# Second attention of an audio tower: another order on TensorE, ScalarE and VectorE, with the values' product in two halves

## The chip, the cores and the metric

The kernel runs on one core of one Trainium2 chip. The metric is the device time of one execution in microseconds (us), from the host's timing of the chip; a profile of one execution gives the spans below. TensorE (PE) does the matmuls, VectorE (DVE) and ScalarE (ACT) read its results from PSUM, GpSimd (POOL) works on SBUF alone, and SyncE (SP) issues DMAs.

## The reference, cut to what matters

The whole kernel computes tokens from 16 signals, and two layers of attention and experts on them. The change lies in the second attention, which for 16 batches (`Bb`) of 255 tokens (`Nn`), 64 channels and 8 heads of 8 channels computes:

```python
qk = (x @ Wqk.T).reshape(Bb, Nn, 2, Hh, hd)
q = qk[:, :, 0].transpose(0, 2, 1, 3)
k = qk[:, :, 1].transpose(0, 2, 1, 3)
patch_score = jax.nn.softmax(jnp.einsum('bhnd,bhmd->bhnm', q, k) * scale, axis=-1)
...
attn = (1.0 - g) * patch_score + g * pos_score[None]
...
v = (x @ Wv.T).reshape(Bb, Nn, Hh, hd).transpose(0, 2, 1, 3)
out = jnp.einsum('bhnm,bhmd->bhnd', attn, v)
out = out.transpose(0, 2, 1, 3).reshape(Bb, Nn, Cc)
return out @ Wproj.T + bproj
```

The softmax over the positions (`pos_score`) does not depend on the tokens; its product with the values is worked out ahead of the loop.

## The kernel before

The second attention (`attention1_and_experts1`) goes through 64 units of work. A unit is one pair of heads of one batch; four units make a batch, two batches one pass of the loop on each engine. Nothing schedules them: each engine has a function `slot`, called once per unit, that says in what order the engine does its part, and semaphores join the engines. A slot on TensorE works on several units at once, each at another stage. The four slots of a batch are slot 0 to 3 (`p` in the code), and a slot's own unit is U. On TensorE a slot before the change is, in this order:

- **scores** (line 1557) of unit U + 1, four matmuls into one pair of PSUM banks, after VectorE has taken the maxima of unit U out of them;
- **turned scores** (line 1563) of unit U - 1, with keys on the partitions, from queries that carry the maxima as extra rows; ScalarE then takes their exponential (line 1920);
- **stack** (line 1551): the queries and keys of unit U + 3 gathered by six matmuls; ScalarE copies them out (lines 1894, 1896);
- **turned maxima** (line 1616) of unit U. VectorE adds them to the queries (line 2095);
- in slots 1 and 3 **outputs** (line 1573): exponentials times values for two units, contracted over 128 and then 127 keys, 16 matmuls in the records (float32 goes in two), in column tiles of 32; ScalarE copies them out in slots 0 and 2 (line 1914);
- in slot 3 the **batch's end**: the projection of the batch before (line 1579) and the **turned outputs** of this one (line 1585);
- in slot 2 the **turned blend** (line 1639) and the **next projection**, which makes queries and keys of the batch after next (line 1545).

VectorE's slot is: maxima of unit U + 1 (line 2062), the sum of queries and turned maxima of unit U (2095), the high and low parts of the new maxima (2071, 2072). Slot 1 adds statistics for a later normalisation (447 to 455), slot 3 a rest of queries and keys (2058) and the batch's end: reciprocals of the turned outputs' sums (2108, 2109), the blend (2112), and the sum with the projection (2119). The turned maxima share PSUM bank 7 with the turned outputs, so they wait in slot 0 until the blend has read those (`s_otr`).

Of the kernel before, what the change touches and what calls it, by code (L numbers as in the profile page):

```python
# [17 lines left out]
ALU = mybir.AluOpType  # L18
# [7 lines left out]
P = 128  # L26
# [8 lines left out]
D = WIN  # L35
# [52 lines left out]
def tower(nc, x, taps, consts, w_raw, gate_b0, w1_01, b1_0, w2_0, b2_0, gamma,  # L88
          split_sel, wpos, wproj, bproj, b1_1, w2_1, b2_1, out):
    with ExitStack() as ctx:  # L90
# [1350 lines left out]
        def attention1_and_experts1(block, e0):  # L1441
# [93 lines left out]
            def _(pe):  # L1535
# [45 lines left out]
                def outputs_turn(b, par):  # L1581
# [4 lines left out]
                    last.then_inc(s_OT, 1)  # L1586

                def slot(j, k, do=("unit", "turned", "pv", "tail")):
# [6 lines left out]
                    if "unit" in do and (not known or U + 1 < UNITS):  # L1595
# [3 lines left out]
                        scores(k + 1)  # L1599
                    if "turned" in do and (not known or U >= 1):  # L1600
# [10 lines left out]
                    if "unit" in do:  # L1611
                        pe.wait_ge(s_mhl, U + 1)
                        if p == 0 and (not known or b >= 2):
                            pe.wait_ge(s_otr, b - 1)
                        for tq in range(2):
                            last = nc.tensor.transpose(MT[:, P * tq:P * tq + P], mhl[k % 2][:, tq], ident_b[:])
                        last.then_inc(s_mtp, 1)
                    if "pv" in do and p % 2 == 1 and (not known or U >= 3):
# [131 lines left out]
                with pe.Fori(1, B // 2 - 1) as j:  # L1750
# [138 lines left out]
            def _(act):  # L1889
# [14 lines left out]
                def slot(j, k, do=("unit", "exp", "o")):  # L1904
# [3 lines left out]
                    b = 2 * j + par  # L1908
                    if p % 2 == 0 and (not known or b >= 1) and "o" in do:
# [5 lines left out]
                    if "exp" in do and (not known or U >= 1):  # L1915
# [593 lines left out]
```

## Time and profile before

| what | value |
|---|---|
| device time, median of 3 runs | 746.05 us (745.96 to 749.63) |
| span of the profiled execution | 745.7 us |
| TensorE busy in the span | 652.7 us (88%) |
| VectorE busy | 570.2 us (76%) |
| ScalarE busy | 502.8 us (67%) |
| GpSimd busy | 334.1 us (45%) |

The span runs from the first to the last instruction of the profiled execution; the median lies 0.35 us above it. The shares are over the whole kernel; the second attention is the stretch from about 494 to 660 us, and only there does an instruction move.

### The profile page before, as it was taken

Reading aid. Unit: us, or ns where it says so; the run is one execution under the profiler, and the core shown is the slowest. Engines: PE = TensorE matmul, PEld = TensorE weight load, DVE = VectorE, ACT = ScalarE, POOL = GpSimd, SP = SyncE. Lnnn points to the kernel's source line nnn. Section 1 sums busy time; section 2 is a strip of 40 time slices with the busy share of each in tenths; the row PEclk is TensorE's granted clock in tenths of the full one; section 3 lists DMA queues with packets and bytes.
Section 4 is the critical chain, followed back from the end, with each engine's and each line's share of the span. In section 5 each row is a group of like instructions: output and inputs, shape, how many; then the busy total and the mean of one; then the engine's idle time right before and its main releaser. Section 6 shows DMA issues by size and latency. Waiting matters only on the chain.

```text
span 745.7 us, 16401 instructions
## 1 busy us (share of the span) xinstructions
PE 652.7 (88%) x4984; PEld 364.3 (49%) x4984; DVE 570.2 (76%) x1633; ACT 502.8 (67%) x1264; POOL 334.1 (45%) x417
## 2 busy tenths in 40 slices
PE   5528998999999988999999997699888988889896
PEld 5514654666666654323333324365555655565332
DVE  6676787777777774798999988669888888867653
ACT  3746877888888872576777767658777777744542
POOL 1006578788787875133333333725445644320000
PEclk9857999999999997999999999699999999987999
DMA  4030000000000001433333330000000000000001
GB/s 109 1 113 1 1 2 1 0 0 0 0 0 0 1 0 66 161 106 108 109 113 115 107 109 14 3 1 2 1 0 0 0 0 0 1 1 1 16 20 23
DMA packets 22038, 24.37 MB, mean 33 GB/s; under 512 B 12390, under 2 KB 12902, under 8 KB 21734
## 3 DMA queue, kind: packets, MB, share of 16 engines
q1 hardware_dynamic: 19751, 23.31, 10.3%
q10 hardware_dynamic: 2239, 0.49, 0.3%
q8 instruction: 22, 0.36, 0.2%
q14 instruction: 26, 0.21, 0.1%
HBM read 22.48 MB, written 1.31 MB: 32 GB/s over the span
## 4 chain that ended last, share of the span: by engine, by line
PE 59%; DVE 19%; issue 8%; ACT 4%; POOL 2%; DMA 1%; DVEq 0%; SPq 0%; ACTq 0%; POOLq 0%
PE ps L723 8%; PE ps L759 7%; PE ps L1551 5%; PE ps L641 4%; PE ps L1573 4%; PE ps L717 4%; DVE big L1091 4%; PE ps L652 3%; DVE big L2062 3%; DVE big L1132 2%; PE ps L1557 2%; PE ps L1802 2%; PE ps L709 2%; PE ps L1824 2%; PE ps L705 2%
## 5 line engine op out<-in xcount | busy, mean ns | idle before, releaser
L1338 POOL TENSOR_TENSOR big<-big 128x1024 f32<-128x1024 f32 x64 | 119.9, 1895 | 45.3 <-DVE big L1152 45.3
L939 ACT ACTIVATE big<-ps,big 128x255 f32<-128x255 f32 x256 | 117.3, 485 | 11.4 <-DVE big L1146 8.9
L901 ACT ACTIVATE big<-ps,b1s 128x512 f32<-128x512 f32 x128 | 80.3, 679 | 40.1 <-PE ps L641 38.9
L1146 DVE TENSOR_REDUCE big<-ps 128x4 f32<-128x1020 f32 x64 | 75.2, 1213 | 27.3 <-PE ps L717 27.3
L1920 ACT ACTIVATE big<-ps 128x1024 f32<-128x1024 f32 x64 | 65.9, 1030 | 32.9 <-PE ps L1563 30.5
L2062 DVE TENSOR_REDUCE big<-ps 128x4 f32<-128x1020 f32 x64 | 78.1, 1220 | 6.8 <-DVE res L2119 2.5
L723 PE MATMUL ps<-cst,big 128*128 128x128 f32 x512 | 77.5, 285 | 6.3 <-POOL big L1338 2.4
L1158 DVE COPY mid<-ps 128x512 f32<-128x512 f32 x96 | 63.5, 686 | 18.7 <-PE ps L723 15.4
L641 PE MATMUL ps<-big,wall 64*128 64x512 f32 x256 | 75.7, 656 | 0.7 <-ACT big L872 0.7
L723 PEld LDWEIGHTS ps<-cst,big 128*128 128x128 f32 x512 | 54.9, 141 | 40.8 <-issue 20.8
L652 PE MATMUL ps<-big,w2s 128*64 128x512 f32 x256 | 70.8, 632 | 1.2 <-ACT big L901 1.2
L759 PE MATMUL ps<-mid,big 128*64 128x256 f32 (+1 forms) x512 | 69.5, 392 | 0.0
L1132 DVE SCALAR_TENSOR_TENSOR big<-ps,b2s,mid 128x512 f32<-128x512 f32 x64 | 48.0, 750 | 21.2 <-DMA mid<-spread_w 7.7
L939 ACT ACTIVATION_READ_ACCUMULATOR big<-ps,big 128x1 f32 x256 | 55.7, 217 | 0.0
L465 POOL TENSOR_TENSOR big<-big 128x4 f32<-128x4 f32 x16 | 16.3, 1016 | 85.6 <-DVE big L455 85.6
L1551 PE MATMUL ps<-big,selqk 128*128 128x256 bf16 x384 | 52.8, 273 | 0.7 <-ACT big L1896 0.4
L1091 DVE TENSOR_TENSOR big<-big 128x512 f32<-128x512 f32 x56 | 44.1, 788 | 0.0
L927 ACT ACTIVATE big<-ps 128x512 f32<-128x512 f32 x64 | 35.0, 602 | 11.1 <-PE ps L705 8.9
L460 POOL TENSOR_TENSOR mid<-mid 128x2 f32<-128x2 f32 x16 | 11.5, 718 | 66.5 <-DVE mid L455 66.5
L1551 PEld LDWEIGHTS ps<-big,selqk 128*128 128x128 bf16 x384 | 32.8, 97 | 17.2 <-issue 13.5
L1557 PE MATMUL ps<-big 64*128 64x256 bf16 x256 | 25.4, 273 | 17.8 <-DVE big L2062 17.7
L759 PEld LDWEIGHTS ps<-mid,big 128*64 128x64 f32 (+1 forms) x512 | 31.1, 136 | 18.7 <-issue 7.9
(274 smaller groups left out, 1342.2 us busy)
## 6 DMA issues: line engine op xcount, KB each, us to landing
mid<-spread_w SPq DMA_DIRECT2D x128, 128.0 KB, 2.8
mid<-in_split_sel SPq DMA_DIRECT2D x1, 1536.0 KB, 7.5
wall<-in_w SPq DMA_DIRECT2D x1, 1280.0 KB, 6.2
out_tokens<-res SPq DMA_DIRECT2D x16, 56.0 KB, 1.6
cst<-in_consts SPq DMA_DIRECT2D x1, 520.5 KB, 5.1
pexp<-in_w_raw SPq DMA_DIRECT2D x1, 512.0 KB, 6.2
w2s<-in_w SPq DMA_DIRECT2D x1, 512.0 KB, 3.4
mid<-in_taps ACTq DMA_DIRECT2D x1, 320.0 KB, 3.9
```

What stands on the lines that cost most here:

```text
L641: last = nc.tensor.matmul(H1(e, j), wst[0][half, f:f + P], xc[q][half], start=True, stop=True)
L652: last = nc.tensor.matmul(Y(e)[D * j:D * j + D], w2s[0][:, 2 * e + j], hid[e % 2][j], start=True, stop=True)
L723: last = nc.tensor.transpose(AT[:, j, c, P * tq:P * tq + P], e_sb[r % 4][:, j, tq, P * c:P * c + P], ident)
L759: last = nc.tensor.matmul(O[D * j:D * j + D, par], val[par][0:n, c, D * h:D * h + D], a_sb[r % 4][0:n, j, c], start=(g == 0 and a == 0 and ...
L901: last = nc.scalar.activation(hid[e % 2][j], H1(e, j), ACT.Relu, bias=b1s[0][:, 2 * e + j:2 * e + j + 1])
L939: last = nc.scalar.activation(e_sb[r % 4][:, jj, tq, 0:NW], S[:, 2 * (r % 2) + jj, tq, 0:NW], ACT.Exp, scale=-1.0, bias=minus[r % 4][:, jj ...
L1091: ins = nc.vector.tensor_tensor(acc[q], acc[q], part[e % 2], ALU.add)
L1146: nc.vector.tensor_reduce(minus[r % 4], S[:, 2 * a:2 * a + 2, :, 0:NW], AX.X, ALU.min).then_inc(s_mx, 1)
L1338: nc.gpsimd.tensor_tensor(e_sb[r % 4], e_sb[r % 4], bc(inverse[r % 4].unsqueeze(3), [P, 2, 2, 256]), ALU.mult).then_inc(s_A, 1)
L1551: last = nc.tensor.matmul(out_, selqk[:, 2 * p + n, part], parts[par][:, part], start=(part == 0), stop=(part == 2))
L1920: nc.scalar.activation(e_sb[(k - 1) % 4], T, ACT.Exp, scale=scale).then_inc(s_E, 1)
L2062: nc.vector.tensor_reduce(mx[k % 2], S[:, :, :, 0:NW], AX.X, ALU.max).then_inc(s_max, 1)
```

## The change

On TensorE the turned maxima go from behind the stack to between scores and turned scores, except in slot 1. The outputs product is cut into its two contractions: the first 128 keys in slots 1 and 3, the other 127 in the slot behind. The batch's end goes from slot 3 to slot 0 of the next batch, behind the second half; the turned maxima of slot 1 are done last in their slot and wait for the blend. On VectorE the batch's end goes from the end of slot 3 to slot 1, between the maxima and the sum with the queries, and the rest of queries and keys goes behind the parts. On ScalarE the copy of the outputs goes from ahead of the exponential to behind it. TensorE's loop starts one pass later; that pass is written out.

```diff
@@ TensorE @@
-                def outputs(k):
+                def outputs(k, c):
...
                     g = p // 2
-                    for c in range(2):
-                        n = P - c
-                        for i in range(4):
-                            last = nc.tensor.matmul(O[32 * i:32 * i + 32, g], v1[par][0:n, c, 4 * g + i], e_sb[(k + i // 2) % 4][0:n, i % 2, c],
-                                                    start=(c == 0), stop=(c == 1))
-                    last.then_inc(s_PV, 1)
+                    n = P - c
+                    for i in range(4):
+                        last = nc.tensor.matmul(O[32 * i:32 * i + 32, g], v1[par][0:n, c, 4 * g + i], e_sb[(k + i // 2) % 4][0:n, i % 2, c],
+                                                start=(c == 0), stop=(c == 1))
+                    if c == 1:
+                        last.then_inc(s_PV, 1)
...
+                def batch_end(b, par):
+
+                    if not isinstance(b, int) or b + 2 < B:
+                        pe.wait_ge(s_rest, b + 3)
+                    if not isinstance(b, int) or b >= 2:
+                        projected(b)
+                    if not isinstance(b, int) or b <= B:
+                        outputs_turn(b, par)
+
+                def max_turn(U, k):
+                    pe.wait_ge(s_mhl, U + 1)
+                    if not isinstance(U, int) or U >= 1:
+                        pe.wait_ge(s_qm, U)
+                    for tq in range(2):
+                        last = nc.tensor.transpose(MT[:, P * tq:P * tq + P], mhl[k % 2][:, tq], ident_b[:])
+                    last.then_inc(s_mtp, 1)
...
                         scores(k + 1)
+                    if "unit" in do and p != 1:
+                        max_turn(U, k)
                     if "turned" in do and (not known or U >= 1):
...
-                        outputs(k - 3)
-                    if p == 3 and (not known or b >= 1) and "tail" in do:
-                        if not known or b + 2 < B:
-                            pe.wait_ge(s_rest, b + 3)
+                        outputs(k - 3, 0)
+                        if known and U >= UNITS - 1:
+                            outputs(k - 3, 1)
+                    if "pv" in do and p % 2 == 0 and (not known or 4 <= U < UNITS):
+                        outputs(k - 4, 1)
+                    if p == 1 and "unit" in do:
+                        if not known or b >= 2:
+                            pe.wait_ge(s_otr, b - 1)
+                        max_turn(U, k)
+                    if p == 0 and "unit" in do and (not known or b >= 2):
+                        pe.wait_ge(s_qm, U + 1)
+                        batch_end(b - 1, 1 - par)
+                    if known and p == 3 and b >= B - 1 and "tail" in do:
                         if "unit" in do:
                             pe.wait_ge(s_qm, U + 1)
-                        if not known or b >= 2:
-                            projected(b)
-                        if not known or b <= B:
-                            outputs_turn(b, par)
+                        batch_end(b, par)
...
@@ ScalarE @@
+                    if "exp" in do and (not known or U >= 1):
+                        act.wait_ge(s_T, U)
...
+                        nc.scalar.activation(e_sb[(k - 1) % 4], T, ACT.Exp, scale=scale).then_inc(s_E, 1)
                     if p % 2 == 0 and (not known or b >= 1) and "o" in do:
...
-                        nc.scalar.activation(e_sb[(k - 1) % 4], T, ACT.Exp, scale=scale).then_inc(s_E, 1)
@@ VectorE @@
                             maxima(U + 1, k + 1)
-                        if p == 3 and (not known or b + 2 < B):
-                            remains(b + 2, par)
+                        if p == 1 and (not known or b >= 2):
+                            batch_end(b - 1)
+                        if p == 1 and (not known or b >= 3):
+                            dve.wait_ge(s_fin, b - 2)
                         dve.wait_ge(s_mtp, U + 1)
...
                             max_parts(U + 1, k + 1)
+                        if p == 3 and (not known or b + 2 < B):
+                            remains(b + 2, par)
...
-                    if p == 3 and (not known or 1 <= b <= B):
-                        dve.wait_ge(s_OT, b)
-                        link(nc.vector.reciprocal(rinv, by_head[:, :, :, HS - 1]))
...
-                        dve.wait_ge(s_fin, b - 1)
+                    if known and p == 3 and b >= B - 1:
+                        batch_end(b)
```

The next two pieces are TensorE's instructions around the batch's end in a pass of the loop, with their semaphores (`L1_` and the name of what has been done). Before, from the outputs of slot 3 to the first matmul of the stack of slot 0:

```order
L1573 MATMUL ps<-big,mid 32x256 [waits L1_outputs_in_sbuf,L1_values_padded]
L1573 MATMUL ps<-big,mid 32x256 x7
L1579 MATMUL ps<-wps,big 128x128 [waits L1_blend_in_sbuf,L1_q_with_max,L1_qk_rest]
L1582 REGISTER_ALU
L1585 MATMUL ps<-cst,big 128x128 [waits L1_outputs_in_sbuf]
L1585 MATMUL ps<-cst,big 128x128 x3
L1557 MATMUL ps<-big 128x256 [waits L1_max,L1_k_in_sbuf,L1_q_in_sbuf]
L1557 MATMUL ps<-big 128x256 x3
L1563 MATMUL ps<-big 128x256 [waits L1_exps,L1_q_with_max]
L1563 MATMUL ps<-big 128x256 x3
L1608 REGISTER_ALU
L1551 MATMUL ps<-big,selqk 128x256 [waits L1_k_in_sbuf,L1_q_in_sbuf]
```

The outputs (1573) stand whole in slot 3, the batch's end (1579, 1585) behind them; in slot 0 the turned scores (1563) follow the scores (1557), and the turned maxima come later, behind the stack (1551).

After, slot 0 behind its scores, up to the turned outputs (the lines of the same work are 1602 for the turned maxima and 1572 for outputs):

```order
L1602 MATMUL ps<-ident_b,big 128x128 [waits L1_q_with_max,L1_max_parts]
L1602 MATMUL ps<-ident_b,big 128x128
L1563 MATMUL ps<-big 128x256 [waits L1_exps,L1_q_with_max]
L1563 MATMUL ps<-big 128x256 x3
L1627 REGISTER_ALU
L1551 MATMUL ps<-big,selqk 128x256 [waits L1_k_in_sbuf,L1_q_in_sbuf]
L1551 MATMUL ps<-big,selqk 128x256 x5
L1572 MATMUL ps<-big,mid 32x256 x4
L1579 MATMUL ps<-wps,big 128x128 [waits L1_blend_in_sbuf,L1_qk_rest,L1_q_with_max]
L1582 REGISTER_ALU
L1585 MATMUL ps<-cst,big 128x128 [waits L1_outputs_in_sbuf]
L1585 MATMUL ps<-cst,big 128x128 x3
```

The turned maxima now stand ahead of the turned scores, half of the outputs (four of the eight instructions) behind the stack, and the batch's end (1579, 1585) in slot 0 with a wait for VectorE's sum (`L1_q_with_max`).

After, slot 1 behind its scores, up to the turned maxima of slot 2:

```order
L1563 MATMUL ps<-big 128x256 [waits L1_exps,L1_q_with_max]
L1563 MATMUL ps<-big 128x256 x3
L1627 REGISTER_ALU [waits L1_parts_ready]
L1551 MATMUL ps<-big,selqk 128x256 [waits L1_k_in_sbuf,L1_q_in_sbuf]
L1551 MATMUL ps<-big,selqk 128x256 x5
L1635 ISA [waits L1_exps]
L1572 MATMUL ps<-big,mid 32x256 [waits L1_outputs_in_sbuf]
L1572 MATMUL ps<-big,mid 32x256 x3
L1602 MATMUL ps<-ident_b,big 128x128 [waits L1_q_with_max,L1_max_parts,L1_turned_outputs_read]
L1602 MATMUL ps<-ident_b,big 128x128
L1557 MATMUL ps<-big 128x256 [waits L1_max,L1_k_in_sbuf,L1_q_in_sbuf]
L1557 MATMUL ps<-big 128x256 x3
```

Here the turned maxima (1602) stand last and wait for the blend (`L1_turned_outputs_read`); the scores of slot 2 and their turned maxima follow at once.

VectorE before, from the parts in slot 3 to the first maxima of the next batch's slot 0:

```order
L2071 TENSOR_TENSOR big<-big 128x4 [waits L1_max_turned,L1_max]
L75 REGISTER_ALU
L2072 TENSOR_TENSOR big<-big 128x4 [waits L1_dve]
L2108 RECIPROCAL big<-ps 128x16 [waits L1_outputs_turned]
L2109 TENSOR_TENSOR big<-big,tail 128x16 [waits L1_dve]
L75 REGISTER_ALU
L2111 REGISTER_ALU [waits L1_dve]
L2112 TENSOR_TENSOR big<-ps,big 128x128 [waits L1_blend_turned]
L2119 ISA [waits L1_projected]
L2119 TENSOR_TENSOR res<-res,ps 128x128
L2061 REGISTER_ALU [waits L1_added]
L2062 TENSOR_REDUCE big<-ps 128x4 [waits L1_scores]
```

The maxima (2062) of slot 0 wait behind the batch's end.

After, slot 1 from its maxima to the first of the parts:

```order
L2082 TENSOR_REDUCE big<-ps 128x4 [waits L1_scores]
L2106 ISA
L2107 RECIPROCAL big<-ps 128x16 [waits L1_outputs_turned]
L75 REGISTER_ALU
L2108 TENSOR_TENSOR big<-big,tail 128x16 [waits L1_dve]
L75 REGISTER_ALU
L2110 REGISTER_ALU [waits L1_dve]
L2111 TENSOR_TENSOR big<-ps,big 128x128 [waits L1_blend_turned]
L2118 ISA [waits L1_projected]
L2118 TENSOR_TENSOR res<-res,ps 128x128
L2135 TENSOR_TENSOR big<-big,ps 128x256 [waits L1_turned_scores,L1_max_turned,L1_added]
L2091 TENSOR_TENSOR big<-big 128x4 [waits L1_max_turned,L1_max]
```

The five instructions of the batch's end (2107 to 2118, before 2108 to 2119) stood ahead of the maxima (2062) of a slot 0; they now stand behind the maxima (2082) of slot 1 and ahead of the sum with the queries (2135).

## Rows read from the trace of the kernel before

**Rows 1.** Busy us (count) of PE, PEld, DVE, ACT, POOL; clock; DMA: one batch.

```profile
599.17:609.45 10.28, 9.10 (x106) 5.97 (x107) 8.99 (x29) 7.75 (x16) 4.98 (x9) 1.00 0.00 0
```

**Rows 2.** Chain that ended last: scores of slot 1, first and last of thirteen.

```profile
515.88 0.40 PE ps L1557 x4
...
640.60 0.40 PE ps L1557 x4
```

**Rows 3.** Timeline, TensorE, one batch from slot 1: start, us, line, shape, count [idle before].

```profile
599.17 0.40 PE L1557 MATMUL ps<-big 64*128 64x256 bf16 x4 [1.49 <-DVE big L2062]
599.39 0.40 PE L1563 MATMUL ps<-big 64*128 64x256 bf16 x4
599.72 0.83 PE L1551 MATMUL ps<-big,selqk 128*128 128x256 bf16 x6
600.39 0.28 PE L1616 MATMUL ps<-ident_b,big 128*128 128x128 bf16 x2
600.59 1.07 PE L1573 MATMUL ps<-big,mid 128*32 128x256 f32 x16
601.60 0.40 PE L1557 MATMUL ps<-big 64*128 64x256 bf16 x4
...
602.81 0.28 PE L1616 MATMUL ps<-ident_b,big 128*128 128x128 bf16 x2
602.92 0.28 PE L1639 MATMUL ps<-cst,big 128*128 128x128 f32 x1
603.04 0.49 PE L1545 MATMUL ps<-big,w 128*128 128x256 bf16 x3
603.46 0.40 PE L1557 MATMUL ps<-big 64*128 64x256 bf16 x4
...
605.93 0.49 PE L1579 MATMUL ps<-wps,big 128*128 128x128 f32 x2
606.25 0.60 PE L1585 MATMUL ps<-cst,big 128*128 128x128 f32 x4
606.78 0.40 PE L1557 MATMUL ps<-big 64*128 64x256 bf16 x4
```

**Rows 4.** Timeline, VectorE, the same batch.

```profile
599.61 1.22 DVE L2062 TENSOR_REDUCE big<-ps 128x4 f32<-128x1020 f32 x1
600.75 0.28 DVE L2095 TENSOR_TENSOR big<-big,ps 128x256 bf16<-128x256 bf16 x1
...
601.15 0.18 DVE L2072 TENSOR_TENSOR big<-big 128x4 bf16<-128x4 f32 x1
601.30 0.36 DVE L447 BATCH_NORM_STATS2 mid<-res 128x6 f32 x2
...
602.09 1.22 DVE L2062 TENSOR_REDUCE big<-ps 128x4 f32<-128x1020 f32 x1
...
606.89 0.26 DVE L2108 RECIPROCAL big<-ps 128x16 f32<-128x16 f32 x1 [0.61 <-PE ps L1585]
...
607.48 0.29 DVE L2112 TENSOR_TENSOR big<-ps,big 128x128 f32<-128x128 f32 x1
607.69 0.28 DVE L2119 TENSOR_TENSOR res<-res,ps 128x128 f32 x1
608.09 1.22 DVE L2062 TENSOR_REDUCE big<-ps 128x4 f32<-128x1020 f32 x1
```

**Rows 5.** Timeline, the last batch: scores of slot 1, then a wait, last turned scores.

```profile
650.70 0.40 PE L1557 MATMUL ps<-big 64*128 64x256 bf16 x4 [1.01 <-DVE big L2062]
...
654.63 0.28 DVE L2095 TENSOR_TENSOR big<-big,ps 128x256 bf16<-128x256 bf16 x1
...
654.96 0.40 PE L1563 MATMUL ps<-big 64*128 64x256 bf16 x4 [1.50 <-DVE big L2095]
...
657.36 0.40 PE L1563 MATMUL ps<-big 64*128 64x256 bf16 x4
```

**Rows 6.** Busy us by stretch, as rows 1: behind the second attention.

```profile
668.00:676.00 8.00, 8.00 (x35) 7.24 (x36) 6.16 (x43) 1.45 (x4) 0.71 (x1) 0.50 0.00 0
```

More of the change, by code:

```diff
@@ L1610, in slot @@
                         stack(at(k + 3)[0], at(k + 3)[1])
[L1611 to L1617, printed above, removed]
                     if "pv" in do and p % 2 == 1 and (not known or U >= 3):
@@ L1749, in _ @@
                     slot(0, k)
-                with pe.Fori(1, B // 2 - 1) as j:
+                for k in range(2 * PAIRS):
+                    slot(1, k)
+                with pe.Fori(2, B // 2 - 1) as j:
                     for k in range(2 * PAIRS):
@@ L2080, in scale_twice, with batch_end @@
                     dve.wait_ge(s_nx, b + 1)
+                def batch_end(b):
+                    known = isinstance(b, int)
+                    if not known or 1 <= b <= B:
+                        dve.wait_ge(s_OT, b)
+                        link(nc.vector.reciprocal(rinv, by_head[:, :, :, HS - 1]))
+                        link(nc.vector.tensor_tensor(rgate, rinv, omg, ALU.mult))
+                        if not known or b >= 2:
+                            dve.wait_ge(s_oTp, b - 1)
+                        nc.vector.tensor_tensor(blend.rearrange("p t (h d) -> p t h d", h=H), by_head[:, :, :, 0:HS - 1],
+                                                bc(rgate.unsqueeze(3), [P, 2, H, D // H]), ALU.mult).then_inc(s_otr, 1)
+                    if not known or b >= 2:
+                        if known and b == 2:
+                            dve.wait_ge(s_biased, CH)
+                        dve.wait_ge(s_y, b - 1)
+                        rs = res[:, span(2 * (b - 2), 2)]
+                        nc.vector.tensor_tensor(rs, rs, Y, ALU.add).then_inc(s_fin, 1)
                 def slot(j, k, do=("unit",)):
@@ L2105, in slot @@
                         scale_twice(b - 3)
-                    if p == 3 and (not known or 1 <= b <= B):
-                        dve.wait_ge(s_OT, b)
-                        link(nc.vector.reciprocal(rinv, by_head[:, :, :, HS - 1]))
-                        link(nc.vector.tensor_tensor(rgate, rinv, omg, ALU.mult))
-                        if not known or b >= 2:
-                            dve.wait_ge(s_oTp, b - 1)
-                        nc.vector.tensor_tensor(blend.rearrange("p t (h d) -> p t h d", h=H), by_head[:, :, :, 0:HS - 1],
-                                                bc(rgate.unsqueeze(3), [P, 2, H, D // H]), ALU.mult).then_inc(s_otr, 1)
-                    if p == 3 and (not known or b >= 2):
-                        if known and b == 2:
-                            dve.wait_ge(s_biased, CH)
-                        dve.wait_ge(s_y, b - 1)
-                        rs = res[:, span(2 * (b - 2), 2)]
-                        nc.vector.tensor_tensor(rs, rs, Y, ALU.add).then_inc(s_fin, 1)
-                        dve.wait_ge(s_fin, b - 1)
+                    if known and p == 3 and b >= B - 1:
+                        batch_end(b)
                 def values_out(c):
```

8 lines of the change are left out of this document (4 added, 4 removed).

## The prediction

> **What bounds the kernel now.** I read the busy time by stretch first, then the chain that ended last, then TensorE's and VectorE's instructions in order of time, and last the end of the stage. In one batch of the second attention, 10.28 us, TensorE is busy 9.10, VectorE 8.99 and ScalarE 7.75, at a granted clock of 1.00 (2.4 GHz) [rows 1]. So TensorE and VectorE each have little over 1 us spare, and the batch is as long as it is because the two wait for each other. The chain shows the pace: from the scores at 515.88 to the same scores twelve batches later at 640.60 are 124.72 us, **10.39 per batch** [rows 2]. Where the waiting lies is in the next two views. TensorE stood 1.49 us for VectorE before the scores at 599.17, and from there to 606.78 shows no wait [rows 3]. VectorE stands 0.61 until the outputs are turned, then does the batch's end from 606.89, and only then, at 608.09, begins the next maxima [rows 4]. The next scores need those maxima's result, so TensorE pays for the batch's end. What could be gained is this wait, 1.49 us here.
>
> The four slots of a batch are numbered 0 to 3, as in the section on the kernel; rows 3 begin with slot 1.
>
> **A price that the steps need: changing the tile shape.** TensorE's rows carry the shape (64\*128, 128\*128, 128\*32). Start to start, equal shapes follow at streaming pace: scores to turned scores 0.22, turned maxima to turned blend 0.11, turned blend to projection of the next batch 0.12. Where the shape changes, about 0.1 is added: turned scores to stack 0.33 against 0.22; turned maxima to outputs 0.20 against 0.11; the three matmuls of the next batch's projection to scores 0.42 against three times 0.11; the turned outputs to scores 0.53 [rows 3]. I take **0.10 per change**. The Trainium skill has a rule that speaks against this change: TensorEngine Tiling (Array Packing), section Key Properties, says that a change of tiling mode (not only of tile) drains TensorE. The rows agree with a cost per change. That page has no price; TensorE: Matmul & The Clock Gate, section Step-by-step: what each phase is for, gives about 128 cycles for the last column to leave the array, and its section on LDWEIGHTS 107 ns for 128 columns, so an estimate from the skill would be 0.16 per change, and the sum below would be about 8 us higher by it.
>
> **The change, walked through one batch.** Zero is the start of the scores in slot 1; all steps are start to start. From rows 3: scores to a 128-row shape 0.32 (0.22 and a change), turned maxima to turned scores 0.21 (0.11 and a change), turned scores to stack 0.33, stack to half an outputs product 0.77 (0.67 and a change), the half to anything else 0.56 (the whole takes 1.01 with one change, so 0.46 and a change), projection 0.32, turned outputs 0.53, turned blend 0.12, next projection 0.42.
>
> Slot 1. TensorE: scores, turned scores, stack, half, ending at 0.22 + 0.33 + 0.77 + 0.56 = 1.88. Then it must turn the maxima, and now waits until VectorE has read the turned outputs. VectorE: maxima from 0.44, the next instruction 1.14 later (599.61 to 600.75), so the batch's end starts at 1.58; reciprocal to blend 0.59, blend 0.29 long: read at 2.46 [rows 4]. A VectorE result releases TensorE after 0.05 (sum of queries and maxima 654.63 to 654.91, turned scores at 654.96 [rows 5]): the maxima are turned at **2.51**, 0.63 after TensorE was free. This is the old wait's successor. Behind it on TensorE stand the scores, turned scores and stack of slot 2.
>
> Slot 2. TensorE's scores at 2.72, ready for the turned maxima at 3.04. VectorE adds the maxima to the queries once they are turned (0.28 long, 0.05 to release: 2.84), ends their high and low parts 0.40 + 0.18 later [rows 4], 3.42; TensorE turns them at **3.47**, another 0.43 lost. VectorE's statistics then start at 3.39 and the maxima 0.79 later [rows 4], at 4.18, ready for TensorE at 4.18 + 1.22 + 0.14 = 5.54 (0.14 from the maxima at 608.09, 1.22 long, to the scores at the boundary 609.45 of the window [rows 1, 4]). TensorE needs 0.21 + 0.33 + 0.77 + 0.56 + 0.12 + 0.42 = 2.41, so slot 3 begins at **5.88**: TensorE is the later one.
>
> Slot 3: 0.32 + 0.21 + 0.33 + 0.77 + 0.56 = 2.19, to **8.07**. Slot 0 of the next batch: 0.32 + 0.21 + 0.33 + 0.77 + 0.56 + 0.32 + 0.53 = 3.04, to **11.11**. VectorE meanwhile has 1.80 to do per slot (0.44 + 1.22 + 0.14) and is early in both, so the wait of 1.49 is indeed gone; but slots 0 and 3 are now TensorE's own work, with four or more changes in each where two or three stood. ScalarE's moved copy of outputs waits for the second half, but ScalarE has 10.28 - 7.75 = 2.5 us spare [rows 1], so I cost it, GpSimd's add (4.98 busy [rows 1]) and the longer code (the first passes of the loop are written out) at nothing; without that cover the copy is priced below.
>
> **The sum.** A batch goes from 10.39 to 11.11: +0.72, twelve times, **+8.6**. The batch after (640.60 to 650.70, 10.10 [rows 2, 5]) has no projection of a next batch: by the same steps slot 3 begins at 5.56, the batch is 10.79, **+0.7**. The last batch takes 657.36 - 650.70 = 6.66 to its last turned scores [rows 5]. With the change VectorE's maxima there start at 4.18 as above, their parts end at 5.90, TensorE turns them at 5.95, then turned scores, both halves, projection, turned outputs, 0.21 + 0.33 + 1.01 + 0.32 + 0.53: 8.35, **+1.7**. The first two batches have no batch's end and come out within 0.1. Total +11.0. The span is 745.7 and the median 746.05, 0.35 around it; with that unchanged the forecast is **757 us**.
>
> **The rivals.**
> *Faster.* TensorE loads the next weights ahead whatever their shape, as long as it has work queued, and a change then costs nothing. Sixteen changes stand on the path from 3.47 to 11.11. Without them slot 3 begins at 5.54 (VectorE is the later one there), slot 3 takes VectorE's 1.80 and slot 0 takes 0.22 + 0.11 + 0.22 + 0.67 + 0.46 + 0.32 + 0.43 = 2.43: 9.77 per batch, -0.6 twelve times, +1 at the end: about 740 us. Against it: from 599.17 to 606.78 TensorE has work queued all the time, and each change costs its 0.1 [rows 3]. It comes out under the time before only if a change costs under 0.04.
> *No change.* Eleven of the sixteen changes are new (five stand in rows 3 already). If the new ones hide and the old ones do not, slot 3 begins at 5.58, slots 3 and 0 take 1.80 and 2.64: 10.02 per batch, -0.4 twelve times, +1.3 at the end: 743; if half of the new ones hide, 10.55 per batch and about 750.
> *Slower still.* The copy of outputs stands ahead of the copies of queries and keys on ScalarE; if it waits longer than my walk says, the next stack waits too. A wait of 0.27 in two slots of thirteen batches is +7: about 764.
> *The clock.* The stage behind runs at 0.50 (1.2 GHz) for long after the sparse end of this one [rows 6]; a longer sparse end may move this by a few us either way. It widens the range.
>
> **Chances.** Slower as worked out 0.66, slower still 0.11, no change 0.13, faster 0.10. A measurement of this kernel tells about 0.5% (3.7 us) from no change. So faster 0.10, same 0.13, slower 0.77. The range leaves out the faster case and the far end of slower still: 746 to 764. If slower as worked out holds, 751 to 763.
>
> **What would show it.** Right: the wait before the scores of slot 1 gone; 0.4 to 0.7 before the turned maxima of slots 1 and 2, released by VectorE's blend and parts; turned maxima between scores and turned scores with 0.32 and 0.21 to their neighbours; 11.0 to 11.2 from batch to batch; VectorE idle about 0.7 us more per batch. Wrong: scores to turned maxima at 0.22, or a batch of under 10.4, would bear out the faster rival; a stack that waits for ScalarE, the slower one.

## The result, and the profile after

After takes 765.69 us (759.10 to 771.07, 4 runs), before in the same comparison 746.76 us (745.96 to 749.63, 4 runs): ratio **1.0234** (95% interval 1.0190 to 1.0277). The four runs spread over 12 us with the granted clock of the whole kernel (0.954 in the fastest, 0.931 in the slowest, which the ratio leaves out). The change makes the kernel slower, as forecast, but by 17.5 us at that ratio (18.9 between the medians) and not by 11. The profiled execution took 764.48 us, its span is 761.7 us, 16.0 longer than before's 745.7.

First the busy time of one batch, from the scores of slot 1 to the same scores of the next batch, the answer to [rows 1]. The columns are busy us (count) of PE, PEld, DVE, ACT and POOL, then TensorE's granted clock, DMA share and GB/s.

```profile
606.73:617.99 11.26, 10.28 (x108) 5.16 (x108) 8.65 (x27) 7.91 (x18) 5.01 (x9) 1.00 0.00 0
```

TensorE is busy 10.28 us of 11.26, where it was 9.10 of 10.28: the same products, with the outputs in more pieces, at the same clock, keep it busy 1.18 us longer, and 0.98 is idle still. Now TensorE's instructions in that batch, the answer to [rows 3] (start, us, line, shape, count, idle time before and what ended it):

```profile
606.73 0.40 PE L1557 MATMUL ps<-big 64*128 64x256 bf16 x4
...
609.24 0.29 PE L1602 MATMUL ps<-ident_b,big 128*128 128x128 bf16 x2 [0.57 <-DVE big L2111]
609.45 0.39 PE L1557 MATMUL ps<-big 64*128 64x256 bf16 x4
610.26 0.28 PE L1602 MATMUL ps<-ident_b,big 128*128 128x128 bf16 x2 [0.41 <-DVE big L2092]
...
612.72 0.40 PE L1557 MATMUL ps<-big 64*128 64x256 bf16 x4
613.05 0.28 PE L1602 MATMUL ps<-ident_b,big 128*128 128x128 bf16 x2
613.27 0.40 PE L1563 MATMUL ps<-big 64*128 64x256 bf16 x4
...
614.93 0.40 PE L1557 MATMUL ps<-big 64*128 64x256 bf16 x4
...
617.99 0.40 PE L1557 MATMUL ps<-big 64*128 64x256 bf16 x4
```

The wait of 1.49 us before the scores of slot 1 is gone. Two others stand in its place: 0.57 before the turned maxima of slot 1, released by the blend (L2111), and 0.41 before those of slot 2, released by the parts (L2092). From slot 3 on nothing waits; there the chain of waits too runs along TensorE alone. VectorE in slot 1, the answer to [rows 4]:

```profile
607.17 1.22 DVE L2082 TENSOR_REDUCE big<-ps 128x4 f32<-128x1020 f32 x1 [1.15 <-PE ps L1557]
...
608.89 0.29 DVE L2111 TENSOR_TENSOR big<-ps,big 128x128 f32<-128x128 f32 x1
...
609.62 0.29 DVE L2135 TENSOR_TENSOR big<-big,ps 128x256 bf16<-128x256 bf16 x1 [0.24 <-PE ps L1602]
```

Now it is VectorE that stands 1.15 us for TensorE's scores. Over the batch it is idle 2.61 us (11.26 - 8.65), where it was 1.29 before: 1.32 more. 0.33 of that is the low part of the maxima, which took 0.51 us before, beside GpSimd's work (605.77), and takes 0.18 here.

The pace, which was 124.72 us for twelve batches [rows 2], is read here from the scores of slot 1 in TensorE's timeline: the batch that begins at 516.21, the one behind it, and the last but one.

```profile
516.21 0.40 PE L1557 MATMUL ps<-big 64*128 64x256 bf16 x4
...
528.28 0.40 PE L1557 MATMUL ps<-big 64*128 64x256 bf16 x4
...
651.58 0.40 PE L1557 MATMUL ps<-big 64*128 64x256 bf16 x4
```

135.37 us for the twelve, +10.65. The first takes 12.07, the other eleven 123.30, or 11.21 each. What the first meets is in the timeline of its slots 1 and 2:

```profile
518.95 0.29 DVE L2135 TENSOR_TENSOR big<-big,ps 128x256 bf16<-128x256 bf16 x1 [0.38 <-PE ps L1602]
519.06 2.77 POOL L2377 TENSOR_TENSOR res<-res,bprojb 128x256 f32<-128x256 f32 x4
519.16 0.66 DVE L2091 TENSOR_TENSOR big<-big 128x4 bf16<-128x4 f32 x1
519.85 0.65 DVE L2092 TENSOR_TENSOR big<-big 128x4 bf16<-128x4 f32 x1
...
520.56 0.28 PE L1602 MATMUL ps<-ident_b,big 128*128 128x128 bf16 x2 [1.31 <-DVE big L2092]
```

VectorE's two parts take 0.66 and 0.65 us instead of 0.17 and 0.18 while GpSimd adds a bias (L2377, four additions in 2.77 us), and TensorE's turned maxima wait 1.31 for them. In the kernel before, the same additions slowed the parts as much (0.69 and 0.65 at 515.85), but the turned maxima stood behind the stack there and came 0.2 later than else (scores of slot 1 to those of slot 2 in 2.63, in the next batch 2.42).

Last the end of the stage, the answer to [rows 5] and [rows 6]: busy time by stretch, and TensorE's timeline of the last batch.

```profile
664.00:665.00 1.00, 0.01 (x1) 0.01 (x1) 0.93 (x5) 0.26 (x1) 0.00 (x0) 1.00 0.00 0
665.00:666.00 1.00, 0.60 (x6) 0.22 (x6) 0.72 (x6) 0.00 (x0) 0.45 (x1) 1.00 0.00 0
666.50:667.00 0.50, 0.50 (x11) 0.20 (x8) 0.47 (x2) 0.33 (x1) 0.23 (x1) 0.51 0.00 0
...
670.00:672.00 2.00, 2.00 (x16) 1.10 (x9) 0.00 (x0) 0.38 (x1) 0.00 (x0) 0.50 0.00 0
672.00:673.00 1.00, 1.00 (x8) 0.48 (x6) 0.21 (x1) 0.00 (x0) 0.00 (x0) 0.50 0.00 0
...
680.60:697.40 16.80, 16.80 (x72) 12.56 (x72) 13.28 (x98) 4.84 (x9) 1.66 (x3) 0.51 0.01 1
```

```profile
662.57 0.40 PE L1557 MATMUL ps<-big 64*128 64x256 bf16 x4
...
664.99 0.28 PE L1602 MATMUL ps<-ident_b,big 128*128 128x128 bf16 x2 [1.24 <-DVE big L2111]
...
668.37 0.40 PE L1602 MATMUL ps<-ident_b,big 128*128 128x128 bf16 x2 [0.33 <-DVE big L2092]
668.69 0.61 PE L1563 MATMUL ps<-big 64*128 64x256 bf16 x4
669.24 1.93 PE L1572 MATMUL ps<-big,mid 128*32 128x256 f32 x16
...
672.68 0.61 PE L1563 MATMUL ps<-big 64*128 64x256 bf16 x4
674.78 1.07 PE L1572 MATMUL ps<-big,mid 128*32 128x256 f32 x16 [1.49 <-ACT big L1940]
```

TensorE stands still for 1.24 us in the last batch, is busy for 0.60 us of the microsecond from 665, and from 666.5 to 673 the granted clock is 0.50 (1.2 GHz): its last products run at half the clock, inside the attention. The last batch takes 10.11 us (662.57 to 672.68) where it took 6.66. In the kernel before, the clock stayed at 1.00 to the end of its last batch, at 657.36. The stretch at half clock in the stage behind is as long as before: here 680.6 to 697.4, there 664.6 to 681.3.

**Where the 16.0 us of span went.** To the scores of slot 1 of the batch at 516.21, from the first scores of slot 0 (495.06): 21.15 against 19.45, +1.70. The twelve batches: +10.65. The batch behind them: 10.99 against 10.10, +0.89. The last batch: +3.45. From its last turned scores to the last outputs: 2.10 (672.68 to 674.78) against 1.52, +0.58. Sum 17.3. The attention begins 1.37 earlier (495.06 against 496.43), which is not the change's doing: over the profiles of this document that start lies anywhere from 491.66 to 496.55. What stands behind the attention is 0.1 longer. 17.3 - 1.4 + 0.1 = 16.0.

### The profile page after: what moved, and what is told of

Read it like the earlier page. It is cut to its first block, busy times and chain, and to the rows that moved or that the text cites. A ratio compares the mean times of both kernels' runs of the same rounds, so it can differ in the third digit from the quotient of the medians.

```text
span 761.7 us, 16427 instructions
## 1 busy us (share of the span) xinstructions
PE 670.7 (88%) x4984; PEld 354.0 (46%) x4984; DVE 566.2 (74%) x1633; ACT 503.8 (66%) x1264; POOL 334.4 (44%) x417
## 3 DMA queue, kind: packets, MB, share of 16 engines
HBM read 22.48 MB, written 1.31 MB: 31 GB/s over the span
## 4 chain that ended last, share of the span: by engine, by line
PE 58%; DVE 18%; issue 9%; ACT 5%; POOL 2%; DMA 2%; SPq 0%; DVEq 0%; ACTq 0%; POOLq 0%
PE ps L723 8%; PE ps L759 7%; PE ps L1551 5%; PE ps L717 4%; PE ps L1572 4%; DVE big L1091 4%; PE ps L641 3%; PE ps L1563 2%; DVE big L1132 2%; PE ps L652 2%; PE ps L1557 2%; PE ps L1602 2%; PE ps L705 2%; PE ps L1844 2%; PE ps L709 2%
## 5 line engine op out<-in xcount | busy, mean ns | idle before, releaser
L641 PE MATMUL ps<-big,wall 64*128 64x512 f32 x256 | 73.6, 640 | 0.7 <-ACT big L872 0.7
L652 PE MATMUL ps<-big,w2s 128*64 128x512 f32 x256 | 69.0, 617 | 1.5 <-ACT big L901 1.2
L1572 PE MATMUL ps<-big,mid 127*32 127x256 f32 (+1 forms) x512 | 41.8, 402 | 1.5 <-ACT big L1940 1.5
L717 PE MATMUL ps<-big 32*128 32x256 f32 x512 | 37.6, 408 | 2.9 <-ACT big L939 1.7
```

The source lines that it names most:

```text
L641: last = nc.tensor.matmul(H1(e, j), wst[0][half, f:f + P], xc[q][half], start=True, stop=True)
L652: last = nc.tensor.matmul(Y(e)[D * j:D * j + D], w2s[0][:, 2 * e + j], hid[e % 2][j], start=True, stop=True)
```

## The experiments

Before, run beside them, took 746.10 us in the comparison of the first four experiments, 743.91 in that of the next four and 744.46 in that of the last. Per batch means from scores of slot 1 to scores of slot 1, and twelve batches means the stretch that took 124.72 us before. M is the new place of the turned maxima on TensorE, H the two halves of the outputs with ScalarE's copy behind the exponential, B the batch's end in the next batch with VectorE's part of it, and what goes with it (the turned maxima of slot 1 last in their slot, the rest of queries and keys behind the parts, the pass that is written out).

| kernel | ratio to before (95%) | twelve batches, us | head, us | last batch, us |
|---|---|---|---|---|
| before | 1 | 124.72 | 19.45 | 6.66 |
| after (M, H, B) | 1.0234 (1.0190 to 1.0277) | 135.37 | 21.15 | 10.11 |
| M alone | 1.0160 (1.0085 to 1.0236) | 133.39 | 21.18 | 6.97 |
| H alone | 1.0021 (0.9990 to 1.0052) | 126.62 | 19.87 | 6.67 |
| B alone | 1.0110 (1.0075 to 1.0144) | 129.34 | 19.81 | 7.90 |
| H and B (after without M) | 1.0111 (1.0028 to 1.0194) | 128.61 | 19.94 | 7.90 |
| M and B (after without H) | 1.0254 (1.0197 to 1.0311) | 132.88 | 21.22 | 10.11 |
| after, TensorE kept busy at the end | 1.0194 (1.0147 to 1.0240) | 135.41 | 21.15 | 8.96 |
| after, GpSimd's bias additions early | 1.0286 (1.0226 to 1.0347) | 134.39 | 21.15 | 10.10 |
| before, sum with projection behind the maxima | 0.9960 (0.9922 to 0.9998) | 118.97 | 19.44 | 6.67 |
| the same, projection in the next slot 0 | 0.9907 (0.9875 to 0.9940) | 116.04 | 19.45 | 6.67 |

Head is the stretch from the first scores of slot 0 to the first of the twelve batches.

Which slots the parts lengthen is read from the same timelines: us from the scores of a slot to those of the next, mean of the eleven batches behind the first of the twelve.

| kernel | slot 1 | slot 2 | slot 3 | slot 0 |
|---|---|---|---|---|
| before | 2.43 | 1.87 | 3.32 | 2.79 |
| M alone | 2.72 | 2.07 | 3.49 | 2.78 |
| H alone | 2.05 | 2.58 | 3.12 | 2.78 |
| B alone | 2.68 | 2.80 | 2.43 | 2.88 |
| H and B | 2.68 | 2.87 | 2.14 | 3.03 |
| M and B | 2.68 | 2.80 | 2.71 | 2.85 |
| after | 2.68 | 3.27 | 2.20 | 3.06 |

**The turned maxima alone (M).** Before, with this edit on TensorE, in all four slots (the change leaves out slot 1):

```diff
+                    if "unit" in do:
+                        pe.wait_ge(s_mhl, U + 1)
...
+                        last.then_inc(s_mtp, 1)
                     if "turned" in do and (not known or U >= 1):
                         pe.wait_ge(s_qm, U)
...
-                    if "unit" in do:
-                        pe.wait_ge(s_mhl, U + 1)
...
-                        last.then_inc(s_mtp, 1)
```

> The kernel before, with one part of the change alone: TensorE turns the maxima between scores and turned scores in every slot; the outputs stay whole and the batch's end stays in slot 3. Theory A (each change of tile shape on TensorE's path costs 0.10 us): two changes more in slots 1, 2 and 3, slot 0 covered by its wait; slots 1 to 3 take 2.7, 2.1 and 3.5 instead of 2.4, 1.9 and 3.3, the batch goes from 10.3/10.6 to 11.0/11.3, the kernel to about 755 us (ratio 1.011 to 1.013). Rival (the loss of the change is the new wait behind VectorE's batch end, the order on TensorE costs nothing): 10.3/10.6 per batch, ratio 0.998 to 1.002.

Measured: 10.95 and 11.25 per batch in turn, 758.70 us. In its timeline of TensorE, the start of slot 0, the start of slot 1, and the scores of slots 2, 3 and 0 read:

```profile
590.94 0.40 PE L1557 MATMUL ps<-big 64*128 64x256 bf16 x4
592.07 0.27 PE L1607 MATMUL ps<-ident_b,big 128*128 128x128 bf16 x2 [0.74 <-DVE big L2114]
...
593.61 0.40 PE L1557 MATMUL ps<-big 64*128 64x256 bf16 x4 [0.18 <-DVE big L2064]
594.01 0.28 PE L1607 MATMUL ps<-ident_b,big 128*128 128x128 bf16 x2
...
596.32 0.40 PE L1557 MATMUL ps<-big 64*128 64x256 bf16 x4
...
598.39 0.40 PE L1557 MATMUL ps<-big 64*128 64x256 bf16 x4
...
601.88 0.40 PE L1557 MATMUL ps<-big 64*128 64x256 bf16 x4
```

In slot 0 the turned maxima now stand in front of turned scores and stack, so these wait for the blend (L2114) as well, 0.74 us, which they did not before. That wait costs nothing: slot 0 takes 2.78 in the mean and took 2.79, since the scores of slot 1 wait for VectorE in both. The loss is in the other three: 2.71, 2.07 and 3.49 us here (593.61 to 601.88), where [rows 3] have 2.43, 1.86 and 3.32. That is two changes of shape more in each, and in slot 1 another 0.07 (scores to turned maxima 0.40 instead of 0.33). Theory A holds, slot for slot, and its rival falls. This part alone costs 8.67 us in twelve batches, and in the head 1.73, as much as the whole change does.

**The two halves alone (H).** The outputs cut in two as in the diff of the change, with ScalarE's copy behind the exponential; nothing else.

> The kernel before, with another part alone: the outputs product in two halves over two slots, ScalarE's copy of the outputs behind the exponential; turned maxima and batch's end stay where they were. Theory A: slots 1 and 3 get shorter by 0.45, slots 2 and 0 longer by 0.56; slot 0 has the old wait as cover, VectorE's maxima hold slot 2: 10.25 to 10.4 per batch, ratio 0.997 to 1.004. Rival (splitting is itself costly: a second change of shape and ScalarE's later copy on the path in both places): 10.7 or more per batch, ratio over 1.006.

Measured: 10.35 and 10.73 per batch in turn, 748.05 us: +1.90 in twelve batches, 10.55 per batch in the mean, and no difference that the times can tell. The ratio is Theory A's, and its interval (up to 1.0052) leaves the rival's out; per batch every second one lies where the rival had it, and the mean lies between the two. Slot 2 gets longer by 0.71 us, although VectorE was to hold it, and slot 3 shorter by 0.20 and not by 0.45; slot 0 stays covered, as Theory A said. Behind the last batch ScalarE's later copy shows:

```profile
660.76 1.07 PE L1572 MATMUL ps<-big,mid 128*32 128x256 f32 x16 [1.49 <-ACT big L1924]
```

The last outputs wait for that copy (L1924) and come 1.88 us behind the last turned scores at a clock of 1.00, where they came 1.52 behind before: 0.36 for the copy.

**The batch's end alone (B).** After, with the outputs whole again and the turned maxima behind the stack, except in slot 1, where they stay last.

> The kernel before, with the third part alone: the batch's end in slot 0 of the next batch on TensorE and in slot 1 on VectorE, the turned maxima of slot 1 last in their slot; outputs whole, turned maxima of the other slots behind the stack. Theory A: the old wait goes, in its place come 0.2 before the turned maxima and 0.4 before the turned scores of slot 2, and slot 3 begins at VectorE's 5.5; 10.7 to 10.9 per batch, ratio 1.005 to 1.009. Rival (the batch's end is the whole loss): 11.1 to 11.3 per batch, ratio 1.014 or more. A third way, that the removed wait counts and nothing takes its place: 9.4 to 9.8, ratio 0.985.

Measured: 10.62 to 11.07 per batch, 10.78 in the mean, 753.65 us. Theory A holds for the batch, and the rival falls; the ratio (1.0110) lies a little above its numbers. Moved without M, the batch's end lengthens the last batch by 1.24 us (7.90), and the clock there stays at 1.00.

**TensorE kept busy at the end.** To tell whether the last batch is long by its order or by the clock: after, with the last batches' stack repeated in the last four slots, results unread.

```diff
+                    if known and "turned" in do and UNITS - 3 <= U <= UNITS:
+                        pe.wait_ge(s_q, UNITS)
+                        pe.wait_ge(s_k, UNITS)
+                        again(2 if U == UNITS else 1)
```

> The changed kernel with four stacks more on TensorE at the end of the second attention (one behind the turned scores of each of the last three units, two behind the very last), written to the same PSUM and read by nobody: work added, none left out. Theory A (the clock fell in the last batch because TensorE did little there): the granted clock stays at 1.00 through the last batch, which takes 8.2 to 8.6 instead of 10.1 to the last turned scores, 2 us are won there, and if the half clock in the next stage goes as well, up to 8 more: 754 to 763. Rival (the clock falls whatever TensorE does there, or on the work of the whole stage): the clock is 0.50 for as long, the time is the changed kernel's 764 or up to 2 more.

Measured: 761.22 us. The windows and the end of the last batch:

```profile
664.00:666.00 2.00, 1.59 (x17) 0.85 (x16) 1.65 (x11) 0.44 (x1) 0.71 (x2) 1.00 0.00 0
666.00:668.00 2.00, 1.84 (x20) 0.71 (x18) 1.46 (x5) 1.22 (x4) 1.90 (x3) 1.00 0.00 0
...
681.50:705.00 23.50, 21.67 (x74) 11.27 (x73) 14.28 (x88) 8.77 (x15) 1.40 (x2) 0.50 0.00 1
```

```profile
661.46 0.40 PE L1557 MATMUL ps<-big 64*128 64x256 bf16 x4
...
667.26 0.28 PE L1608 MATMUL ps<-ident_b,big 128*128 128x128 bf16 x2 [0.15 <-DVE big L2102]
667.48 0.39 PE L1563 MATMUL ps<-big 64*128 64x256 bf16 x4
667.81 0.83 PE L1581 MATMUL ps<-big,selqk 128*128 128x256 bf16 x6
668.56 1.07 PE L1572 MATMUL ps<-big,mid 128*32 128x256 f32 x16
...
670.42 0.40 PE L1563 MATMUL ps<-big 64*128 64x256 bf16 x4
```

With TensorE at work in the gaps the clock stays at 1.00, as Theory A has it, and the last batch takes 8.96 us. Of these 0.75 are the repeated stack at 667.81, which nothing hides (668.56 - 667.48 = 1.08 where 0.33 stood): without it 8.21. So the order costs the last batch 8.21 - 6.66 = 1.55 us and the clock the other 1.90. In the next stage 1.2 GHz lasts here from 681.5 beyond 705, against 16.8 us in after. That the work in the gaps brought this is not shown: the profiled run (766.50 us, span 764.7) is the longest of its four, whose other spans are 757.0 to 760.8, and the first stretch at half clock in that stage lasts 10 to 17 us in the profiles of the other kernels. Nor do the times tell this kernel from after (1.0194 against 1.0234, with intervals that overlap). So it is shown that the half clock lengthens the last batch; that filling the gaps would make the kernel faster is not.

**The sum with the projection behind the maxima.** A version of before, on VectorE alone: reciprocals and blend stay where they were, only their sum with the projection goes behind the maxima of slot 0.

```diff
                     if "unit" in do:
+                        if p == 0 and (not known or b >= 2):
+                            gated(b - 1)
                         if not known or U + 1 < UNITS:
                             maxima(U + 1, k + 1)
+                        if p == 0 and (not known or b >= 3):
+                            added(b - 1)
```

> The kernel before on every engine but VectorE: reciprocals and blend of the batch's end stand at the start of slot 0 (so the loop's branch falls into the wait for the turned outputs), the sum with the projection goes behind slot 0's maxima. Theory A (what VectorE does between the turned outputs and the next maxima sets the batch, since TensorE's next scores wait for those maxima): 0.4 less in each batch and 0.3 more where the loop ends, 9.8 to 10.0 per batch instead of 10.39, the kernel at 739 to 742 us (ratio 0.99 to 0.994). Rival (TensorE's own work or ScalarE holds the batch at 10.3 once VectorE is earlier): 10.2 to 10.4 per batch, ratio 0.998 to 1.002.

Measured: 742.93 us and 9.86 to 10.03 per batch, twelve in 118.97 (-5.75). Per batch Theory A holds; the ratio (0.9960) lies a little above its 0.99 to 0.994, with an interval that just leaves out 1. VectorE's work between the turned outputs and the scores of slot 1 is on the path that sets the end of a batch; taking 0.4 us out of it is a gain in every batch, and moving the whole of it was not.

**GpSimd's bias additions early.** After, with the additions of L2377 put ahead of GpSimd's loop, to tell whether they cost the head and the batch at 516.21.

```diff
+                for c in range(CH):
+                    add_bias(c)
                 for b in range(B):
                     slots(b, b % 2)
...
-                    if b < 2:
-                        for c in range(CH // 2 * b, CH // 2 * b + CH // 2):
-                            add_bias(c)
```

> The changed kernel with GpSimd's eight additions of the projection's bias ahead of its batch loop instead of behind its first two batches. Theory A (VectorE's parts take 0.66 instead of 0.17 in slot 2 of batch 2 because GpSimd's additions run then, and the change has put them on the path): batch 2 takes 11.2 instead of 12.07, the first eleven units 0.5 to 1.5 less, the kernel 1.5 to 2.5 us less than the changed one. Rival (the first pass is slow for another reason, as the code that is now written out): batch 2 at 12.07 still, no difference.

Measured: the batch at that place takes 11.11 us instead of 12.07; its parts read

```profile
517.17 0.17 DVE L2091 TENSOR_TENSOR big<-big 128x4 bf16<-128x4 f32 x1
517.37 0.18 DVE L2092 TENSOR_TENSOR big<-big 128x4 bf16<-128x4 f32 x1
```

That 0.96 us is shown to be GpSimd's. The head stays at 21.15, where Theory A had 0.5 to 1.5 less: its 1.7 us are not GpSimd's. In the head the longest wait of TensorE is, in after and here, another:

```profile
506.62 0.82 PE L1551 MATMUL ps<-big,selqk 128*128 128x256 bf16 x6 [0.69 <-ACT big L1916]
```

This line of after is a stack that waits 0.69 us for ScalarE, the sign that the prediction gave for its slower rival; here the same wait ends at 504.63. From 516.21 on the timeline of after shows no stack that waits. The time does not show the gain (764.65 us, four runs between 760.23 and 769.95).

**After without M, and after without H.** Each is after with one part undone as in the kernels above.

> The changed kernel with the turned maxima behind the stack again in slots 0, 2 and 3; halves and moved batch's end stay. Theory A (changes of shape on the path, waits as walked): 10.5 to 10.8 per batch, ratio to before 1.004 to 1.01. Rival (the parts' losses add up, each alone 0.16 and 0.38 over before): 10.9 to 11.0 per batch.

Measured: 10.50 to 11.08 per batch, 10.72 in the mean, 755.80 us, last batch 7.90 at a clock of 1.00. Theory A holds per batch, and the rival falls. Without M, 6.8 of the 10.65 us in twelve batches, 1.2 of the head's 1.7 and 2.2 of the last batch's 3.45 are gone.

> The changed kernel with the outputs product whole in slots 1 and 3 and ScalarE's copy ahead of the exponential again; order of the turned maxima and moved batch's end stay. Theory A: slot 1 has the whole product in its wait, slot 3 begins at VectorE's 5.5: 10.9 to 11.05 per batch, ratio to before 1.012 to 1.018. Rival (the parts' losses add up, each alone 0.72 and 0.38 over before): 11.4 to 11.5 per batch.

Measured: 10.99 and 11.06 per batch for most, 762.56 us. Theory A holds per batch, and the rival falls (11.03 in the mean behind the first batch); the ratio (1.0254) lies above its numbers, which had no half clock in the last batch. That batch takes 10.11 with the half clock in it, so in these profiles the fall comes with M and B together, and H is not needed for it.

**The projection in the next slot 0.** On top of the fifth kernel: its trace still has 0.69 to 0.78 us of idle time before the scores of slot 1, and the projection stands ahead of the turned outputs. It goes into that idle time.

```diff
                         last.then_inc(s_mtp, 1)
+                        if p == 0 and (not known or b >= 3):
+                            projected(b - 1)
...
-                        if not known or b >= 2:
+                        if known and b >= B - 1:
                             projected(b)
+                        elif not known or b >= 2:
+                            pe.wait_ge(s_oT, b - 1)
```

> The kernel of the fifth experiment (sum with the projection behind slot 0's maxima on VectorE, 9.86 to 10.03 per batch), and on TensorE the projection taken out of slot 3 and put into slot 0 of the next batch, behind its turned maxima, where the trace of the fifth has 0.69 to 0.78 of idle time before the next scores. Theory A (what is left of the old wait is the way from the turned outputs over reciprocal, blend and maxima to the scores of slot 1, and the projection stands ahead of the turned outputs on it): turned outputs, reciprocal, blend, maxima and scores all come about 0.33 earlier, the projection costs nothing in the idle time: 9.55 to 9.65 per batch, span about 4 us less than the fifth's 738.0, ratio to before 0.985 to 0.992. Rival (VectorE's own work in slot 3, whose parts end 0.48 before the reciprocal, is next in the way, or the added projection pushes the scores): a batch of 9.75 to 9.95 and a ratio of 0.992 to 0.997.

Measured: 737.98 us, ratio 0.9907; 9.59 and 9.77 per batch in turn, span 733.9. TensorE's timeline at the end of slot 3 and in slot 0:

```profile
589.02 0.66 PE L1585 MATMUL ps<-cst,big 128*128 128x128 f32 x4
...
590.90 0.28 PE L1616 MATMUL ps<-ident_b,big 128*128 128x128 bf16 x2
591.01 0.44 PE L1579 MATMUL ps<-wps,big 128*128 128x128 f32 x2
591.97 0.40 PE L1557 MATMUL ps<-big 64*128 64x256 bf16 x4 [0.52 <-DVE big L2068]
```

The projection costs nothing behind the turned maxima: slot 0 takes 2.22 us in the mean, 2.21 in the fifth kernel. The ratio and the span, 4.1 us below the fifth's, are Theory A's, though the ratio's interval (up to 0.9940) reaches into the rival's; a batch takes 9.67 in the mean, 0.24 less than the fifth's and not 0.33, and every second one lies in the rival's range, so what holds those is open. 0.52 us are left in this batch of the wait that was 1.49 in [rows 3]. This is the fastest version that ran.

## Why the prediction was wrong in size

**Right: the mechanism and the batch.** The forecast's walk gave the turned maxima of slot 1 at 2.51, of slot 2 at 3.47, slot 3 at 5.88, slot 0 at 8.07, the end at 11.11. Measured from 606.73: 2.51, 3.53, 5.99, 8.20 and 11.26. The old wait is gone and the two new ones stand where it said, released by the instructions that it named. Per batch 11.21 was measured (eleven batches): 0.10 more than 11.11. One sign came out larger: VectorE is idle 1.32 us more per batch, not 0.7.

**Right: the price of a shape.** Scores to turned maxima take 0.33 and turned maxima to turned scores 0.22 (612.72 to 613.27), forecast 0.32 and 0.21. So the faster rival and no change fall at the point that the prediction set for them, 0.32 against 0.22; M alone adds 0.29, 0.20 and 0.17 us to slots 1 to 3 for two changes in each. The page TensorEngine Tiling (Array Packing) of the Trainium skill, section Key Properties, says that a change of tiling mode drains TensorE; these steps agree that each change costs something, and do not show by what. With the 0.16 per change of the prediction's other estimate the sum would have been 765, which is where the time came out, but by chance: a change costs 0.10 to 0.11 in these rows, and the rest came from elsewhere.

**Wrong: the last batch, "+1.7".** The step was worked out at the full clock, and at that clock it was right: 8.35 forecast, 8.21 in the kernel kept busy. In the kernel after, the turned maxima that it put at 5.95 come at 5.80 (668.37); what follows up to the last turned scores was 2.40 in the sum and is 4.31 (668.37 to 672.68), at 1.2 GHz. The clock adds 1.90 to this term. Behind it the last outputs come 0.58 later, which had no term: 0.36 is ScalarE's copy, as in H alone, and the other 0.22 comes with the half clock, as in M and B without H (1.74 against 1.52). The prediction had the clock as a rival that "widens the range" by a few us, and looked for it in the stage behind, whose half clock is as long as before; it fell in the batch itself, after waits of 1.24 us for the blend and 0.41 for the parts. A wait alone does not tell: before has one of 1.50 us in its last batch [rows 5], B alone one of 1.62, both at a clock of 1.00.

**Wrong: "The first two batches have no batch's end and come out within 0.1".** They took 1.70 more. The reason given was beside the point: the turned maxima in front need no batch's end to cost time. M alone has the head at 21.18, H and B alone have it at 19.87 and 19.81, H and B together at 19.94. What holds TensorE there is not the same in each: with M alone the longest wait of the head is 0.75 us for VectorE's parts, after has the 0.69 for ScalarE. That M brings the loss is shown; how much of it each wait makes is open.

**Wrong: GpSimd and ScalarE's copy "at nothing".** The copy costs the 0.36 behind the last batch; in the twelve batches no stack waits for it. GpSimd's bias additions slow VectorE's parts, and in the new order TensorE stands behind those: 0.96 us in the batch at 516.21. The page SBUF — State Buffer of the Trainium skill, section SBUF: two separate sides, says that a VectorE operation with two SBUF inputs and a GpSimd operation that reads SBUF lock each other out for a whole instruction. The rows agree: GpSimd's four additions take 0.69 each, so by the row's start they end at 519.75 and 520.45 (worked out), and the two parts end at 519.82 and 520.50.

**The sum again.** Forecast 8.6 + 0.7 + 1.7 = 11.0. Measured 10.65 + 0.89 + 3.45, and 1.70 and 0.58 that had no term: 17.3. Of the 6.3 us between, 2.1 are the half clock (1.90 and 0.22), 1.7 the head, 1.1 eleven batches at 0.10 too little, 1.0 GpSimd's additions, 0.4 ScalarE's copy; the batch behind the twelve adds 0.2, and the last batch at full clock gives 0.15 back. Less the 1.3 by which the rest of the kernel came out shorter, that is 5.0 of span. The prediction also set the span of before (745.7) beside a median of 746.05 and took 0.35 for what lies around a span; the profiled run with M alone has 1.8 around it (755.93 against 754.1), that of after 2.8 (764.48 against 761.7). That is 1.5 to 2.4 us of the forecast's base; 5.0 and 2.4 make the 7.4 us between the forecast and the profiled run's 764.48.

**What each part costs.** M is the costly one: undone, twelve batches fall by 6.8 us, alone it adds 8.7. B alone adds 4.6, H 1.9. They do not add up (15.2 against 10.65), and the table of slots shows where. Alone, M lengthens slots 1, 2 and 3 by its changes of shape. With B the maxima of slot 1 stay last, so M adds nothing there, and slot 2 is as long with M and B as with B alone (2.80), as TensorE waits there anyway (with B alone 0.56 us before the scores of slot 3). With H as well, slot 2 has more of TensorE's work behind its wait: 3.27, where H and B have 2.87. Against before, after loses 1.40 us in slot 2, 0.25 in slot 1 and 0.27 in slot 0, and wins 1.12 in slot 3. Why a steady batch is 0.1 longer than the walk is not settled; in the batch shown 0.11 of the 0.15 lie in slot 2 (3.27 against 3.16).

## What to carry to other kernels

Where one engine waits for a short chain on another, take out of that chain what does not belong on it (here the sum, then the projection: -5.8 and -2.9 us in twelve batches); moving the whole chain only moved the wait, and put more of TensorE's work behind it. An instruction that is moved ahead makes everything that stands behind it on its engine wait for what it waits for. Ask of each such wait whether the engine would have waited there anyway: the new 0.74 us in slot 0 of M alone cost nothing, with the 0.41 in slot 2 of after that slot is 0.40 longer than without M (3.27 against 2.87). Ask it for the first batches too. Work out the last batch at both clocks: look at the waits of TensorE there, and count what follows at the half clock as a bound.

## What was not expected of the hardware

The granted clock fell to 0.50 (1.2 GHz) inside the attention, by 666.5, after TensorE had been busy 0.01 us of the microsecond from 664 and 0.60 of the next, and stayed there to 673 although TensorE was busy for most of that; with work in those gaps it stayed at 1.00 (2.4 GHz). The same fall stands in the profiles of two other kernels with M and B (last batch 10.10 and 10.11). In the kernel with H and B TensorE was busy 0.00 us of the microsecond from 657 and 0.89 of the next, and the clock stayed at 1.00 through that batch; what tells the two apart is not settled. An operation of VectorE on 4 columns took 0.65 us instead of 0.17 beside GpSimd's additions.
